# A four-layer graph kernel: order of passes in split products, and a re-planned beginning and end

## The reference

```python
# L0: H = (adj != 0), G = D^-1 H B^-1 H^T
h = relu(G @ (x @ W1.T) + b1); h = layer_norm(h, gamma, beta); y = G @ (h @ W2.T) + b2 + x
# L1: relu([x, (adj @ x) / deg] @ W.T)
# L2: x = relu(adj@(x@W1)+b1); x = relu(adj@(x@W2)+b2); out = adj@(x@W3)+b3
# L3: relu((adj @ x) @ kernel) * (any feature of x non-zero)
```

## Time and profile before

| what | value |
|---|---|
| median of 3 runs | 1405.96 us |
| the profiled execution's own time | 1406.28 us |
| its span, first to last instruction | 1404.5 us |
| TensorE busy | 1378.7 us, 98% |
| DVE, ACT, POOL busy | 1135.4, 1126.3, 1013.2 us |
| mean granted TensorE clock | 0.995 of full speed |
| between two G in mid-kernel | 21.30 us |

### The profile page before, as it was taken

One profiled execution on the slowest core, in us unless ns is written; L12 is line 12 of the kernel. 1 busy time (PEld: TensorE's weight loads), 2 busy tenths in 40 slices (PEclk: granted clock), 3 DMA queues, 4 the chain that ended last, 5 costly groups with the idle time before them and its releaser, 6 DMA issues. The chain is left out here.

```text
span 1404.5 us, 35429 instructions
## 1 busy us (share of the span) xinstructions
PE 1378.7 (98%) x10896; PEld 1336.8 (95%) x10896; DVE 1135.4 (81%) x4086; ACT 1126.3 (80%) x2639; POOL 1013.2 (72%) x1065
## 2 busy tenths in 40 slices
PE   7999999999999999999999999999999999999995
PEld 7999999999999999999999999999999999999995
DVE  7888888787887887787887888877878877878886
ACT  6777887887887878878878878778878788788775
POOL 5857778777777787787787787777777877877530
PEclk9999999999999999999999999999999999999998
DMA  4100110101101101101101101011011011010001
GB/s 141 35 21 20 39 36 24 39 30 30 39 20 39 39 21 39 39 20 39 39 20 39 38 21 39 28 32 39 20 39 39 20 39 39 20 39 28 1 16 38
DMA packets 29961, 47.17 MB, mean 34 GB/s; under 512 B 3408, under 2 KB 12240, under 8 KB 29776
## 3 DMA queue, kind: packets, MB, share of 16 engines
q1 hardware_dynamic: 29776, 44.91, 10.1%
HBM read 28.12 MB, written 16.78 MB: 32 GB/s over the span
## 5 line engine op out<-in xcount | busy, mean ns | idle before, releaser
L961 ACT ACTIVATE x<-n_s,n_shift,n_rstd 128x256 f32<-128x256 f32 x384 | 208.4, 591 | 6.5 <-DVE n_shift L1550 5.1
L216 POOL TENSOR_TENSOR r_lo<-r_f,r_hi 128x512 fp32r<-128x512 f32 x122 | 157.7, 1293 | 45.3 <-ACT r_hi L942 40.1
L209 POOL TENSOR_TENSOR h_lo<-h_f,h_hi 128x512 fp32r<-128x512 f32 x122 | 158.1, 1296 | 40.3 <-ACT h_hi L942 40.1
L2111 POOL TENSOR_TENSOR n_s<-tk,mask 128x512 f32<-128x512 f32 x60 | 62.5, 1042 | 141.8 <-DVE mask L1603 135.1
L375 PE MATMUL psum<-v_hi,h_hi 128*128 128x256 f32 x512 | 149.6, 292 | 1.2 <-ACT tk L1123 1.0
L375 PE MATMUL psum<-w2c_hi,r_hi 128*128 128x258 f32 x512 | 145.8, 285 | 0.2 <-issue 0.2
L375 PE MATMUL psum<-w2c_lo,r_hi 128*128 128x258 f32 x512 | 144.5, 282 | 0.0
L375 PE MATMUL psum<-v_hi,h_lo 128*128 128x256 f32 x512 | 144.4, 282 | 0.0
L375 PE MATMUL psum<-gx_hi,w1T_hi 128*128 128x256 f32 x512 | 144.3, 282 | 0.1
L375 PE MATMUL psum<-v_lo,h_hi 128*128 128x256 f32 x512 | 144.1, 282 | 0.0
L1526 DVE BATCH_NORM_STATS2 n_st<-n_s 128x6 f32<-128x256 f32 x384 | 142.1, 412 | 2.2
(11 more groups left out here) (166 smaller groups left out, 5379.8 us busy)
## 6 DMA issues: line engine op xcount, KB each, us to landing
x_in<-x_in_dram SPq DMA_DIRECT2D x64, 256.0 KB, 2.8
out<-x SPq DMA_DIRECT2D x64, 256.0 KB, 2.0
at_in<-adjT SPq DMA_DIRECT2D x64, 128.0 KB, 2.2
x<-v_in SPq DMA_DIRECT2D x3, 256.0 KB, 5.6
n_s<-w2T_in SPq DMA_DIRECT2D x2, 256.0 KB, 3.5
r_f<-w1T_in SPq DMA_DIRECT2D x2, 256.0 KB, 5.5
h_f<-wab_in SPq DMA_DIRECT2D x2, 256.0 KB, 5.9
tk<-wk_in SPq DMA_DIRECT2D x1, 256.0 KB, 5.5
```

The lines of the kernel that those rows point to most:

```text
L209: return e.tensor_tensor(dst[1][:], src, f(dst[0][:]), ALU.subtract).then_inc(signal, 1)
L216: e.tensor_tensor(r_s[1][:, half], r_f[:, half], f(r_s[0][:, half]), ALU.subtract).then_inc(r_lo[h], 1)
L961: last = act.activation(dst[:, g, :], nm.s[:, g, :], ACT.Identity, scale=nm.rstd[:, g:g + 1], bias=nm.shift[:, g:g + 1])
L2111: pool.tensor_tensor(n4.s[:], tk[:], bc(mask[:], [C, 2, D], 2), ALU.mult).then_inc(tk_masked, 1)
```

## The change

1. `product` is replaced by `early` and `late`. `early` issues the two passes of each term that use only the high part of the state; `late` issues the one that uses its low part. The wait for the low part stands between them. In P, XAB and AXB both outputs are done early and then both late; in the others output 0 is done early, then the wait, then late, and then output 1 early and late.
2. H2 moves from bank 3 to bank 0. In the body its wait is for `gt_hi(n)` (Tr's bank read out) in place of `n2.summed`; waits for `gx_lo` and `h2_relu` stand at other places.
3. On ACT `copy_GT(n)` moves ahead of `root_h`, and `round_GT(n)` ahead of `make_x3`. On POOL `low_GT(n)` moves ahead of `low_p`.
4. Each norm has a memset target of its own in `mean_var` (`wait_pad` before).
5. `fill` and `drain` have new orders on all engines and in the input DMA queue, and `moments` and `invert_shift` are written as their parts there, with other work between.

```diff
-BANK = dict(... H2=3, ...)
+BANK = dict(... H2=0, ...)
...
-            def product(o, terms, start=True, stop=True):
-                for t, (a, b) in enumerate(terms):
-                    mm(o, a[0], b[0], start and t == 0, False)
-                    mm(o, a[0], b[1], False, False)
-                    last = mm(o, a[1], b[0], False, stop and t == len(terms) - 1)
-                return last
+            def early(o, terms, state, start=True):
+                for t, ab in enumerate(terms):
+                    a, b = ab
+                    mm(o, a[0], b[0], start and t == 0, False)
+                    mm(o, a[1 - state], b[state], False, False)
+
+            def late(o, terms, state, stop=True):
+                for t, ab in enumerate(terms):
+                    a, b = ab
+                    last = mm(o, a[state], b[1 - state], False, stop and t == len(terms) - 1)
+                return last
...
             def P(p, h):
+                pe.wait_ge(r_hi[h], upto(p))
+                for o, terms in outs:
+                    early(o, terms, 1, start=h == 0)
                 pe.wait_ge(r_lo[h], upto(p))
-                for g in range(2):
-                    product(...)
+                for o, terms in outs:
+                    late(o, terms, 1, stop=h == 1)
...
             def AP3(p):
                 pe.wait_ge(h2w_hi, upto(p))
-                pe.wait_ge(h2w_lo, upto(p))
-                for g in range(2):
-                    last = product(...)
+                for j, (o, terms) in enumerate(outs):
+                    early(o, terms, 0)
+                    if j == 0:
+                        pe.wait_ge(h2w_lo, upto(p))
+                    last = late(o, terms, 0)
...
             def body(n):                                   # TensorE
+                pe.wait_ge(gx_lo, n)
                 R(n - 1, 0)
-                pe.wait_ge(gt_hi, n)
+                pe.wait_ge(h2_relu, n - 3)
                 R(n - 1, 1)
...
                 Gx(n)
-                pe.wait_ge(n2.summed, n - 1)
+                pe.wait_ge(gt_hi, n + 1)
                 H2(n - 3)
...
             def drain():                                   # TensorE, first and last lines
-                pe.wait_ge(h1w_out, 59)
-                pe.wait_ge(n2.shifted, 60)
                 pe.wait_ge(p_made, 61)
-                G(62)
-                pe.wait_ge(gt_hi, 62)
                 R(61, 0)
+                pe.wait_ge(ax3_lo, 58)
+                pe.wait_ge(h1w_out, 59)
+                pe.wait_ge(n2.shifted, 60)
+                G(62)
...
                 # before: H1(63) H2W(62) Ax3(61) H1W(63) AP3(62) H2(63) TK(61) H2W(63) Ax3(62) AP3(63) TK(62) Ax3(63) TK(63)
                 # after:  Ax3(61) H1(63) H2W(62) TK(61) H1W(63) AP3(62) H2(63) H2W(63) Ax3(62) AP3(63) TK(62) Ax3(63) TK(63)
...
             def body(n):                                   # ACT
                 square_mean(n - 1)
+                copy_GT(n)
                 root_h(n - 1)
+                round_GT(n)
                 make_x3(n - 4)
                 round_p(n - 1)
-                copy_GT(n)
                 copy_h1w(n - 3)
                 high_ax3(n - 4)
-                round_GT(n)
                 high_gx(n)
...
             def fill():                                    # DVE, the end of the beginning
                 sum_n3(2)
-                moments(n3, 2)
-                invert_shift(n3, 2)
-                moments(n4, 1)
-                invert_shift(n4, 1)
+                stats(n3, 2)
+                mean_var(n3, 2)
+                stats(n4, 1)
+                invert(n3, 2)
+                mean_var(n4, 1)
+                shift(n3, 2)
+                invert(n4, 1)
+                shift(n4, 1)
                 wide_var(5)
...
             def drain():                                   # DVE, near its end
-                low_ax3(62)
-                count_nonzero(62)
+                count_nonzero(62)
+                mean_var(n4, 61)
+                low_h2w(63)
+                low_ax3(62)
+                invert(n4, 61)
+                shift(n4, 61)
                 sum_n3(63)
```

More of the change, by code:

```diff
@@ L448, in GP @@
             def GP(p):
+                outs = [(psum[:, bank("GP", p), g * D:(g + 1) * D],
+                         [(part(GT_s[p % 2], ALL, g), part(p_s, ALL, g))]) for g in range(2)]
                 pe.wait_ge(p_hi, upto(p))
-                pe.wait_ge(p_lo, upto(p))
                 pe.wait_ge(gt_lo, upto(p))
-                for g in range(2):
-                    last = product(psum[:, bank("GP", p), g * D:(g + 1) * D],
-                                   [(part(GT_s[p % 2], ALL, g), part(p_s, ALL, g))])
+                for j, (o, terms) in enumerate(outs):
+                    early(o, terms, 0)
+                    if j == 0:
+                        pe.wait_ge(p_lo, upto(p))
+                    last = late(o, terms, 0)
                 last.then_inc(pe_did["GP"], 1)
@@ L502, in H1W @@
                     pe.wait_ge(v_lo, 2)
+                outs = by_state("H1W", p, h1_s, v_s[1])
                 pe.wait_ge(h1_hi, upto(p))
-                pe.wait_ge(h1_lo, upto(p))
-                weigh("H1W", p, h1_s, v_s[1])
+                for j, (o, terms) in enumerate(outs):
+                    early(o, terms, 1)
+                    if j == 0:
+                        pe.wait_ge(h1_lo, upto(p))
+                    last = late(o, terms, 1)
+                last.then_inc(pe_did["H1W"], 1)
             def H2(p):
@@ L856, in drain @@
-                pe.wait_ge(n3.summed, 60)
-                AXB(61)
-                pe.wait_ge(n1.done, 63)
                 TK(58)
                 pe.wait_ge(xbw_lo, 62)
-                H2(60)
+                P(63, 0)
+                pe.wait_ge(n3.summed, 60)
+                H1W(60)
+                P(63, 1)
+                pe.wait_ge(h1_relu, 61)
+                H2(60)
+                pe.wait_ge(tk_relu, 59)
+                Ax2(61)
+                pe.wait_ge(n2.summed, 62)
+                Ax3(59)
@@ L862, in drain @@
+                xT(62)
+                squares(63)
+                pe.wait_ge(h1w_out, 61)
+                H2W(60)
+                pe.wait_ge(n1.done, 63)
+                H1(61)
+                pe.wait_ge(ax2_lo, 62)
+                pe.wait_ge(h2_relu, 61)
+                XAB(62)
                 pe.wait_ge(p_made, 64)
                 GP(63)
-                pe.wait_ge(tk_relu, 59)
-                XAB(62)
-                pe.wait_ge(h1w_out, 61)
-                H2W(60)
-                pe.wait_ge(n2.summed, 62)
@@ L869, in drain @@
[L869 to L882 removed]
+                AP3(60)
+                pe.wait_ge(x1T_lo, 63)
@@ L1240, in fill @@
+                high_gx(4)
+                copy_h1w(0)
+                root(n2, 1)
+                round_GT(4)
+                square_mean(3)
+                make_x2(1)
+                relu_h2(0)
+                root_h(3)
+                round_h2(0)
+                root(n1, 2)
+                round_p(3)
                 relu_r(4, 0)
-                relu_h1(0)
-                round_GT(4)
-                round_h1(0)
+                high_x1T(2)
+                high_ax2(1)
                 relu_r(4, 1)
-                root(n2, 1)
@@ L1433, in drain @@
-                root_h(63)
+                relu_h1(60)
+                round_h1(60)
+                make_x4(57)
+                relu_tk(58)
+                round_r(63, 1)
+                copy_A(62)
+                root(n1, 62)
+                root(n2, 61)
+                root(n3, 59)
                 copy_h1w(60)
-                round_p(63)
-                high_x1T(62)
-                relu_tk(58)
+                make_x2(61)
+                make_x3(59)
                 relu_h2(60)
@@ L1994, in drain @@
+                shift(n3, 59)
+                make_x1(62)
+                stats(n4, 58)
+                mean_var(n4, 58)
+                low_h2(dve, 60)
+                low_ax2(61)
+                wide_var(63)
+                count_nonzero(59)
+                invert(n4, 58)
+                shift(n4, 58)
+                make_p(63)
+                low_A(dve, 62)
                 low_x1T(62)
-                moments(n2, 61)
+                low_h2w(60)
+                low_p(dve, 63)
+                low_ax3(59)
```

1136 lines of the change are left out of this document (586 added, 550 removed), and 39 rows, old and new, of the table BANK_OF.

## The result

| | before | after |
|---|---|---|
| median | 1405.68 us, 4 runs | 1394.95 us, 4 runs (1394.88 to 1395.03) |
| the profiled execution's span | 1404.5 us | 1392.9 us |
| period of G in the body | 21.30 us | 21.21 us |

The ratio is 0.9921, with a 95% interval of 0.9904 to 0.9938. The forecast was 1400.2 us, with a range from 1396.5 to 1406.0. The direction was right; the size was not.

What follows compares the result with a forecast made beforehand. TensorE, busy 1378.7 of 1404.5 us, was taken as the bound, with stalls only at the ends. From 1406.28 us: end -2.7, G(62) -1.0, fill -1.3, drain -0.8, body 0, so 1400.5, less 0.3: 1400.2 us; range 1396.5 to 1406.

Steps and rivals of the forecast that it cites:

- Part 6: ACT's new order and H2's bank in the body: 0 us taken, bounds -4.2 and +5.0.
- Rival D: Body: early copy of GT frees Gx by 0.06 per iteration, late iterations vanish: 4.2 us more gain, 1396; chance 0.08.
- rival A: Body: ACT's moved copies delay root_h and make_x3, 0.29 per iteration beyond the slack: 16 us, 1416 us; chance 0.10.
- Part 1 in the body: Low-part waits between passes in the 55 body iterations: 0 us taken, upper bound 61 us of loss.
- rival C: Waits inside products hold weight loads back, 0.08 us each: up to 61 us, 1460; chance 0.04.
- Part 1 in the ends: Last pair's products start from the high part: TK(63) gains 0.7 us, H2W(63) 0.6, AP3(63) 0.5.
- Part 4: Fill: stats(n4) put into n3's round trip to ACT removes the stall before Ax3(2): gain 1.3 us.
- Part 3: Switch to drain: R(61,0) before G(62) covers the wait for n2.shifted: gain 1.0 us.
- Parts 1, 2 and 5: End: three last-pair products earlier, count_nonzero(62) before the low parts (0.9), together 2.7 us; waits for x in mid-drain, 0.8.
- part 5: Middle of drain: half the cost of two waits for a normed x saved, 0.8 us; bounds 0 and 2.2.
- B: Rival: new ends stall in other places, giving back 2.3 us, and the body loses 1.7: 1404.5 us; chance 0.12.

Runs made afterwards that it cites:

- e3_act: Kernel before with only ACT's order in the body changed (copy_GT ahead of root_h, round_GT ahead of make_x3) and POOL's low_GT ahead of low_p: 1404.24 us, 0.9991.
- e4_n2wait: Changed kernel with the wait for n2.summed put back in front of H2, which stays in bank 0: 1397.15 us, 0.9943.
- e8_actbank: Kernel before with ACT's and POOL's new order in the body and H2 in bank 0, passes and waits as before: 1403.01 us, 0.998.
- e5_body: Kernel before with all of the change's edits to the body, beginning and end as before: 1401.84 us, 0.9971.
- d3_last: Changed kernel with the low part's wait in front of the product again, for pair 63 alone: 1400.95 us, 0.9964.
- h3_mid_fill: Kernel before with the new pass order and waits inside the products for pairs 0 to 56, all other orders old: 1403.75 us, 0.9985.
- e6_front: Changed kernel with every wait for a low part back in front of its product, orders and all else as changed: 1411.02 us, 1.0039.
- f1_fill_drain: Changed kernel with DVE's old order of n3(2) and n4(1) in the last fill iteration, and G(62) again before R(61,0): 1398.32 us, 0.9948.
- d2_count: Changed kernel with count_nonzero(62) back behind low_ax3(62) on DVE, directly before sum_n3(63): 1396.28 us, 0.9933.
- e7_p: Changed kernel with P's waits per output, like those of the other products: 1396.19 us, 0.9927.

## Why the prediction was wrong, step by step

**Part 6, the failed step, 5.07 us.** It said "I take 0 for the body" and of H2's bank "it no longer waits for n2.summed, which came in time, ... Cost 0, gain 0". Both halves were wrong in the same way: a wait without idle time was taken for a wait without cost. Gx was held by 0.05 us in every iteration by the late copy of GT (e3_act), and H2 would have been held by n2.summed once Gx was free (e4_n2wait). With that falls the sentence on which the whole sum stands, that "the body can only lose, except for rare late iterations". Rival D had the first mechanism and nearly the size, 0.06, but a chance of 0.08, because "the distance doesn't shrink when TensorE is early". That distance was measured to Gx's mark, and what is late is not the mark but the second of the eight records behind it. The other part of D, that "the late iterations vanish", did not come: they cost some 1.0 us of the 54 periods in the changed kernel as before. The range was also drawn too high for its own argument: it "takes in D's side", but ends at 1396.5, above D's 1396. ACT's order and the bank move give 0.049 a period together, 2.6 us (e8_actbank). The other 0.044, 2.4 us, come with the remaining edits of the body (0.022 by e5_body) and with differences between e5_body and the changed kernel (0.022). What in them does it stays open. The fear about x3's slack, and rival A with it, was empty: with 0.17 us left Ax3 lost nothing.

**Part 1 in the body: right.** The period with waits inside and in front is 21.219 and 21.216. A cost of 0.08 per wait, rival C, is excluded. The Trainium skill ("TensorE: Matmul & The Clock Gate", Step-by-step) says that TensorE pulls the next weight load ahead of matmuls in flight. The loss that I had drawn from it for a wait in between does not come here: across a wait that is satisfied long before, the starts stand 0.12 apart.

**Part 1 in the ends: the mechanism right, its reach missed.** The price of TK(63)'s low part is exactly the 0.72 forecast (d3_last). But the forecast looked for idle time at low parts and found it at three products of the last pair. In the beginning the same edit gives 1.2 to 1.6 us, in pieces too small to be marked (h3_mid_fill), where the forecast has "I take 0, bounds -1.2 and +1.0"; the changed kernel gains 1.54 there. And the new orders can't be had without it (e6_front: 16 us).

**Part 4, `fill`: right.** Forecast 1.3, measured 1.66, and f1_fill_drain loses 1.63 of it again at Ax3(2).

**Part 3, the switch: right.** Forecast 1.0, measured 1.27, and 1.39 in f1_fill_drain.

**Parts 1, 2 and 5 at the end: 3.5 forecast, 1.89 measured.** The rows of the changed kernel that answer to those of before:

```profile
1371.61 0.62 ACT L983 ACTIVATE h_hi<-h_f 128x512 fp32r<-128x512 f32 x1
...
1372.37 0.36 PE L374 MATMUL psum<-v_hi,h_hi 128*128 128x256 f32 x1 [1.72 <-ACT h_hi L983]
...
1375.00 0.36 PE L374 MATMUL psum<-h2w_hi,A_hi 128*128 128x256 f32 x1
...
1376.68 0.69 DVE L1752 TENSOR_TENSOR n_s<-psum,x2c 128x512 f32<-128x512 f32 x1
...
1381.01 1.13 PE L374 MATMUL psum<-A_f,x 128*128 128x128 f32 x8 [3.23 <-ACT x L1002]
...
1382.18 0.60 ACT L983 ACTIVATE ax_hi<-psum 128x512 fp32r<-128x512 f32 x1 [1.12 <-PE psum L374]
1382.92 0.55 PE L374 MATMUL psum<-wk_hi,ax_hi 128*128 128x256 f32 x1 [0.78 <-ACT ax_hi L983]
```

H2W(63) does start from the high part, 0.14 after it, and still no earlier than before, 71.99 us behind G(63) against 71.80. TK(61) no longer stands between H2(63) and H2W(63) but before H1W(63). So H2(63) starts 69.14 us behind G(63) in place of 68.22, and 1.72 us of idle time took TK(61)'s old place. The sum counted what the wait for the low part gives and not what the move of TK(61) takes: AP3(63) starts 0.52 earlier than before, but its late passes wait for the low part, so it ends only 0.1 earlier. That 0.1 is all that came of 0.57 for H2W(63), 0.5 for AP3(63) and part 5's 0.8. That TK(61) could go back behind H2(63) with a gain was not tried; make_x3(62) overwrites the x that the sum behind TK(61) reads, so it would be later too.

sum_n3(63) starts 0.30 us behind AP3(63) in place of 0.93, since count_nonzero(62) is away; d2_count confirms the price with 0.85. Of it 0.5 reach Ax3(63), the forecast said 0.9. TK(63) gives its 0.7. And one term was not in the sum at all: Ax3(63) took 1.72 us before and 1.13 after. Its row in the kernel before:

```profile
1391.30 1.72 PE L375 MATMUL psum<-A_f,x 128*128 128x128 f32 x8 [3.23 <-ACT x L961]
```

The idle time ahead is the same 3.23 us; the fall to the lower of the two clock levels comes inside Ax3(63) before (clock 0.86 in its first 0.5 us, 0.50 in the next) and behind it after (1.00 up to its end, 0.50 in TK(63)). So the 1.89 are 0.58 up to Ax3(63), 0.59 of its own length and 0.72 of TK(63). I had taken the 0.24 a pass of TK(63) as given, and the 1.72 for no sign at all.

**The tests that the forecast set itself.** "The prediction is wrong if the period changes by more than 0.1 us": it changed by 0.09. The period named for D, 21.24, is the nearest. From AP3(63)'s end to the end of the span it is 16.5 us against 18.3, where 1.6 less was forecast; but 0.6 of this is the clock. B's stalls elsewhere are there (1.72 us before H2W(63)), hidden in the total by gains from other places.

## What to carry to other kernels

An engine that shows no idle time can still be held at a handover in every iteration. Compare the length of the group behind a wait, and the distance to the next stage, with the same product where its operand came early: 1.10 against 1.06 us in one row was 2.6 us in the total. When such a hold is removed, ask at once which wait is next by the same few hundredths, because an edit that costs 15 us alone (1421.1 us, the bank move) can add to the gain of another: 1404.2 us with ACT's order alone, 1403.0 with both. The step between these two is within the intervals; it shows in the period, 21.277 and 21.263.

A wait put between the passes of a product was free in this body, where it is satisfied, and saved up to 16 us in ends whose order was planned on it. So it is worth trying in all products, as one edit with the order of the ends. Idle time at the end has a second price in the clock of what follows, which decided between 1.1 and 2.0 us for one product; filling it with matmuls of no use took 1.1 us off the changed kernel's end, and its median is 1.6 us lower, though the intervals of the two ratios overlap.

## What the runs showed of the hardware that was not expected

- A product whose wait ends shortly before its start is marked at its usual time, but its second record comes late (0.16 to 0.17 us behind the first in place of 0.11), so the group takes longer. With n2.summed 0.12 us ahead of H2's mark the group was 0.06 longer, with 0.18 us it was not. For x3, written by ACT, 0.17 us was enough; for GT, also written by ACT, 0.28 us still cost 0.05. ACT's reading of PSUM beside Gx is the less likely cause, since the delay is the one that an added wait alone leaves in e4_n2wait, but no run takes the two apart. Why 0.28 us is not enough for GT while 0.17 is for x3 stays open.
- The granted clock at the end is on an edge. With the same 3.2 us of idle time ahead, Ax3(63) took 1.13, 1.72 or 2.05 us in different kernels. In e7_p the clock dipped already in Ax3(62), behind 1.7 us of idle time and a product, and in the changed kernel, with the same idle time there, it did not. Differences of 1 to 2 us between kernels with other edits can be this alone.
